# Layer b's attention with each head's rows in its own strip of 32 partitions

## The reference

```python
x = x + attn_a(layernorm(x), ...)     # latent K/V, 16 heads of 8, a rotary part of 32
x = x + ffn(layernorm(x), ...)        # 8 experts, top-k per expert
x = x + attn_b(layernorm(x), qkv_weights)
x = x + ffn(layernorm(x), ...)

def attn_b(x, qkv_weights):           # 16 heads of 8, causal
    q, k, v = ...                     # from x @ qkv_weights
    a = einsum('aib,ajb->aij', q, k) / sqrt(8)
    a = softmax(tril * a + -1e9 * (1 - tril))
    return einsum('aij,ajb->aib', a, v)
```

## Time and profile before

| | us |
|---|---|
| time, median of 3 runs | 1124.67 (1121.18 to 1125.11) |
| the profiled execution's own time | 1126.51 |
| its span | 1124.8 |
| mean granted clock of TensorE | 0.929 |
| PE busy / PEld / DVE / ACT / POOL | 982.4 / 666.7 / 745.9 / 696.5 / 228.6 |
| layer b's attention, first product to last transpose | 613.8 to about 907 |

### The profile page before, as it was taken

How to read it: one execution, slowest core, us unless ns; L and a number is a source line. 1 busy time by engine, 2 the same in 40 slices (tenths; PEclk the granted TensorE clock), 3 DMA queues, 4 the chain that set the end, 5 groups by cost and what they waited for, 6 DMA issues and landing times. The chain is left out here.

```text
span 1124.8 us, 15534 instructions
## 1 busy us (share of the span) xinstructions
PE 982.4 (87%) x5476; PEld 666.7 (59%) x5476; DVE 745.9 (66%) x1305; ACT 696.5 (62%) x1163; POOL 228.6 (20%) x488
## 2 busy tenths in 40 slices
PE   1676999999998799989966799999999859998997
PEld 1344565555554577868844455555655447776886
DVE  6565677767751667669872666766767266776996
ACT  1403566666666589868832066666666748986885
POOL 5103445553342000000007022222222200000000
PEclk9956999999999699989988599999999969998999
DMA  3593432443111011365405521222100020116551
GB/s 83 124 241 82 105 90 83 113 113 86 48 40 57 28 38 38 67 156 145 86 0 142 102 29 30 30 29 30 22 9 1 2 75 19 57 36 134 157 125 39
DMA packets 64957, 81.32 MB, mean 72 GB/s; under 512 B 6080, under 2 KB 52976, under 8 KB 64112
## 3 DMA queue, kind: packets, MB, share of 16 engines
q1 hardware_dynamic: 62944, 79.20, 28.8%
q10 hardware_dynamic: 1936, 1.13, 0.4%
HBM read 56.58 MB, written 22.68 MB: 70 GB/s over the span
## 5 line engine op out<-in xcount | busy, mean ns | idle before, releaser
L1158 PE MATMUL f_banks<-f_hr,f_w2r 128*128 128x512 f32 x768 | 194.1, 401 | 10.3 <-DMA f_w2r<-scratch_w 7.7
L1220 ACT ACTIVATE f_h<-f_banks,b_t 128x512 f32<-128x512 f32 x256 | 167.2, 682 | 44.7 <-PE f_banks L1142 42.0
L1142 PE MATMUL f_banks<-f_xr,f_w1r 128*128 128x512 f32 x768 | 193.0, 400 | 0.0
L1273 DVE TENSOR_TENSOR f_hr<-f_h,f_hr 128x1024 fp32r<-128x1024 f32 x128 | 156.2, 1223 | 31.7 <-ACT f_hr L1226 29.9
L904 DVE TENSOR_REDUCE a_mlate<-a_banks 128x2 f32<-128x1024 f32 (+3 forms) x120 | 124.8, 1079 | 68.2 <-PE a_banks L772 52.1
L1158 PEld LDWEIGHTS f_banks<-f_hr,f_w2r 128*128 128x128 f32 x768 | 144.9, 193 | 40.4 <-DMA f_w2r<-scratch_w 8.6
L904 DVE TENSOR_REDUCE b_mlate<-b_banks 128x2 f32<-128x1024 f32 (+3 forms) x120 | 124.8, 1079 | 57.1 <-PE b_banks L772 41.5
L1142 PEld LDWEIGHTS f_banks<-f_xr,f_w1r 128*128 128x128 f32 x768 | 145.3, 193 | 29.0
L1226 ACT ACTIVATE f_hr<-f_h 128x1024 fp32r<-128x1024 f32 x128 | 136.0, 1062 | 4.1
L764 PE MATMUL a_banks<-a_k,a_q 120*128 120x512 f32 (+3 forms) x384 | 108.6, 388 | 26.8 <-POOL a_q L680 9.2
L807 PE MATMUL a_banks<-a_q,a_k 121*128 121x512 f32 (+3 forms) x384 | 117.2, 388 | 8.0 <-DMA a_q<-a_mt 6.2
(11 more groups left out here) (218 smaller groups left out, 1107.2 us busy)
## 6 DMA issues: line engine op xcount, KB each, us to landing
scratch_w<-a_tab SPq DMA_DIRECT2D x16, 512.0 KB, 3.0
f_w1r<-scratch_w SPq DMA_DIRECT2D x16, 512.0 KB, 5.4
f_w2r<-scratch_w SPq DMA_DIRECT2D x16, 512.0 KB, 6.1
v<-scratch_gate SPq DMA_DIRECT2D x32, 256.0 KB, 5.3
xt<-scratch_gate SPq DMA_DIRECT2D x32, 256.0 KB, 5.2
a_rot<-in_w SPq DMA_DIRECT2D x16, 256.0 KB, 4.1
scratch_q<-a_q_hl SPq DMA_DIRECT2D x24, 128.0 KB, 2.8
scratch_k<-a_k_hl SPq DMA_DIRECT2D x24, 128.0 KB, 2.8
```

Source lines behind the costliest of these rows:

```text
L1142: last = pe.matmul(h_ps[:, j, :], w1r[e % 2][:, wp, j * P:(j + 1) * P], xr[xp][:, chunk(c)], start=(i == 0), stop=(i == 2))
L1158: last = pe.matmul(y_ps[:, q % 2, :], w2r[e % 2][:, wp, j * P:(j + 1) * P], hr[q % 2][hp][:, j, :], start=(j == 0 and i == 0), stop=(j == ...
L1220: act.activation(h[q % 2][:, j, :], h_ps[:, j, :], ACT.Gelu, bias=m.b1_t[:, e * HB + j:e * HB + j + 1]).then_inc(gelu_done, 1)
L1273: dve.tensor_tensor(hr[q % 2][1][:, first:end, :], h[q % 2][:, first:end, :], hr[q % 2][0][:, first:end, :].bitcast(F32), ALU.subtract).th ...
```

## The change

Layer b gets its own layout. Each head's 24 rows lie in its own strip of 32 partitions (head h of the group from partition 32h on), with the maximum's row behind them, and a buffer is [128, 1024] for four heads. No zero rows are multiplied. There are eight buffers each for Q and K, one for each group, and four semaphores for their loads (WAYS); a group's load is 8 DMAs of 24 rows. Products of heads in different strips use different row groups of the array. The pieces of both layers are formed as pairs of heads in two banks; the piece of four heads (`quarter`) in layer b runs in two steps of two heads, each with its own masks, and PE waits for the end of the first step before the second (`fenced`). K in layer b is stored in all three slots like Q. `pt` has buffers of its own in layer b, so ACT's waits for the stores go. SP stores batch 1 not in the projection but in `attention_stage.sync` at half 0, behind the maxima rows of half 1, and loads groups 2 and 3, then (when the stores have landed) 4, and later 5, 6 and 7.

```diff
+WAYS = 4
+KB = len(QSLOT) * HD
+def pieces_early(kind):
+    low = lambda h: ([([(h, 2, 0, 384, 0, 0), (h + 1, 2, 0, 384, 1, 0), (h, 0, 0, P, 0, 384), (h + 1, 0, 0, P, 1, 384)],
+                       [(0, 256, P), (1, 256, P)])],
+                     [("two", 0, 384, h, 2), ("two", 384, P, h, 0)])
+    full = lambda h: ([([(h, 3, 0, CH, 0, 0), (h + 1, 3, 0, CH, 1, 0)], [(0, 384, 0), (1, 384, 0)])],
+                      [("two", 0, CH, h, 3)])
+    return [low(0), full(0), quarter(kind, 1, 0, "four"), low(2), full(2)]
+def quarter(kind, q, k0, how):
+    products = [(h, q, k0, 256, h // 2, h % 2 * 256) for h in range(GH)]
+    if kind == "a":
+        steps = [(products, [(0, P, 256), (1, P, 256)])]
+    else:
+        steps = [(products[i::2], [(bank, P + 256 * i, 0) for bank in range(2)]) for i in range(2)]
+    return steps, [(how, 0, 256, 0, q)]
+def pieces_late(kind):
...
+    near = lambda h, q: pair(h, q, 0, [])
+    ends = lambda h: pair(h, 7, CH, [(0, 384, 0), (1, 384, 0)])
...
+    return [near(0, 7), ends(0), tails(0), near(0, 4), near(0, 5), near(0, 6), quarter(kind, 5, CH, "four"),
+            near(2, 7), ends(2), tails(2), near(2, 4), near(2, 5), near(2, 6)]
 def load_group(eng, m, kind, n, loaded):
+    if kind == "b":
+        for side, t in (("k", m.k2[n]), ("q", m.q2[n])):
+            for h in range(GH):
+                eng.dma_start(t[VW * h:VW * h + KB, :].bitcast(F32),
+                              m.scratch[side][n, :, :, h * T:(h + 1) * T].rearrange("s d t -> (s d) t")
+                              ).then_inc(loaded[n % WAYS], 16)
+        return
 # project_stage
-            for i in range(NBUF):
-                link(pool.memset(m.k2[i][:, :, :].bitcast(F32), 1.0))
-                link(pool.memset(m.q2[i][0:R2, :, :].bitcast(F32), 0.0))
+            for t in m.k2:
+                link(pool.memset(t[:, :].bitcast(F32), 1.0))
 # project_stage.sync
+        store_q(sp, 0, range(1, NG), stored_q[0])
+        store_k(sp, 0, range(1, NG), stored_k[0])
         if latent:
+            second_batch(sp)
         sp.wait_ge(stored_q[0], 16 * stores_q[0])
         sp.wait_ge(stored_k[0], 16 * stores_k[0])
         load_group(sp, m, kind, 1, loaded)
+    def second_batch(sp):
+        sp.wait_ge(split, per * NCH)
+        store_q(sp, 1, range(NG), stored_q[1])
+        store_r(sp, 1, stored_k[1])
+        store_k(sp, 1, range(NG), stored_k[1])
 # attention_stage
+        pt = [sb(f"pt_{i}", [P, GH, CH], F32) for i in range(NPT)]
+    def head_rows(t, n, h, columns, with_max):
+        if latent:
+            return t[n % NBUF][0:M0 + with_max, h, columns]
+        return t[n][VW * h:VW * h + KB + with_max, columns]
 # attention_stage.sync
             if i + 1 < NH2:
                 m_rows(sp, i + 1)
+            if i == 0 and not latent:
+                before.second_batch(sp)
+                load_group(sp, m, kind, 2, loaded)
+                load_group(sp, m, kind, 3, loaded)
+                sp.wait_ge(before.stored_q[1], 16 * before.stores_q[1])
                 sp.wait_ge(before.stored_k[1], 16 * before.stores_k[1])
-            if i == LAST[n] and n + NBUF < GROUPS:
+            if not latent:
+                for g in range(WAYS):
+                    if i + 1 == max(FIRST[g], 1):
+                        load_group(sp, m, kind, g + WAYS, loaded)
 # max_piece
+            for step, (products, masks) in enumerate(PIECES[kind][c][x][0]):
+                if step:
+                    fences[0] += 1
+                    last.then_inc(fenced, 1)
+                    pe.wait_ge(fenced, fences[0])
+                for h, q, k0, w, bank, col in products:
+                    last = pe.matmul(to[:, bank, col:col + w], head_rows(q2, n, h, slice(q * P, (q + 1) * P), 0),
+                                     head_rows(k2, n, h, slice(k0, k0 + w), 0), start=True,
+                                     stop=k0 + w != (q + 1) * P, skip_group_check=True)
```

More of the change, by code:

```diff
@@ L63, in set_tiles @@
     return out, col
[L66 to L74, removed]
@@ L77, in pieces_late @@
[L77 to L88, removed]
@@ L93 @@
+PIECES = {kind: [pieces_early(kind), pieces_late(kind)] for kind in "ab"}
+TURN = [(j, len(PIECES["a"][c])) for j, (n, c) in enumerate(HALVES)]
 LEAD = 17000
@@ L205, in loads_of @@
     buffer_groups = range(n % NBUF, n + 1, NBUF)
-    return sum(3 if kind == "b" else 4 if g and rope_load(kind, g) else 2 for g in buffer_groups)
+    return 2 * GH * (n // WAYS + 1) if kind == "b" else sum(4 if g and rope_load(kind, g) else 2 for g in buffer_groups)
 def rope_load(kind, n):
@@ L349, in load_group @@
                           ).then_inc(loaded[n % NBUF], 16)
[L350 to L356, removed]
+        eng.dma_start(t[R2:M0, :, :].bitcast(F32), m.scratch[side][n, :, :, :].rearrange("s d (h t) -> (s d) h t", h=GH)
+                      ).then_inc(loaded[n % NBUF], 16)
 def rope_copies(n):
@@ L585, in project_stage @@
         stage.free, stage.rope_in = (rot_all, tab_all), rope_in
-    stage.copied, stage.split, stage.splits = copied, split, per * NCH
+    stage.copied, stage.split, stage.splits, stage.second_batch = copied, split, per * NCH, second_batch
     return stage
@@ L754, in max_piece @@
             if x == 0 and j == FIRST[n]:
-                pe.wait_ge(loaded[n % NBUF], 16 * loads_of(kind, n))
+                pe.wait_ge(loaded[n % (NBUF if latent else WAYS)], 16 * loads_of(kind, n))
                 if rope_load(kind, n):
@@ L868, in scalar @@
         m_rows(act, 0)
-        for b in range(B):
+        for b in range(B if latent else 0):
             act.wait_ge(before.stored_q[b], 16 * before.stores_q[b])
@@ L955, in project_and_attend @@
 def project_and_attend(nc, ctx, m, a, kind):
-    loaded = [ctx.enter_context(nc.semaphore(f"loaded_{kind}{i}")) for i in range(NBUF)]
+    loaded = [ctx.enter_context(nc.semaphore(f"loaded_{kind}{i}")) for i in range(NBUF if kind == "a" else WAYS)]
     with ExitStack() as local:
         sb = lambda name, shape, dt: local.enter_context(nc.sbuf_tensor(f"{kind}_{name}", shape, dt))
-        m.q2, m.k2 = [[sb(f"{side}2_{i}", [P, GH, T], F32R) for i in range(NBUF)] for side in "qk"]
+        shape, count = ([P, GH, T], NBUF) if kind == "a" else ([P, T], GROUPS)
+        m.q2, m.k2 = [[sb(f"{side}2_{i}", shape, F32R) for i in range(count)] for side in "qk"]
         m.q_hl, m.k_hl = sb("q_hl", [P, 2, B * T], F32R), sb("k_hl", [P, 2, B * T], F32R)
```

133 lines of the change are left out of this document (61 added, 72 removed).

## The result

The changed kernel takes 1188.7 us (median of 4 runs, 1181.8 to 1192.5) against 1122.9 for the kernel before beside it (4 runs, 1121.1 to 1125.1): a ratio of 1.058, 95% interval 1.052 to 1.063, +65.8 us. The forecast was 1123.5 with a range of 1100 to 1148, so the time lies far outside. The profiled execution took 1189.5 us, its span is 1187.8, its mean granted clock 0.840 (0.929 before).

A forecast was written before the change was run, and what follows sets the result against it. PE was taken to set the pace, though not alone. From 1126.5 us profiled, -8.2 for the steady part and +7.0 for SP's queue gave 1125.3; the runs' median being 1.8 lower, 1123.5 us, range 1100 to 1148.

The forecast's parts named there:

- the rival "the clock": Layer b's steady part: emptier PE falls to clock 0.50, +13 us a group, +85 for all; chance 0.05.
- the steady part and its edges: Layer b's attention, 6.5 head groups: -1.8 us a group on PE, 0.7 of it reaching the end, makes -8.2 us.
- the rival in which nothing runs side by side: Layer b's products: no overlap while strips drain, +4.3 us per group, 1151.3 us in all; chance 0.17.
- The price s of a change of strips: Layer b on PE: each change between strips and full height and back costs 0.25 us, 16 per group, 4.0 us.
- the rival with free strips: Layer b on PE: entering strips costs nothing, -5.8 us per group, 1105.3 us in all; chance 0.29.
- The factor 0.7: Layer b's steady part: 0.7 of each microsecond off PE reaches the end, the rest is paid back in waits.
- PE's sum of -1.8 us per group: Layer b's head group on PE: +0.66 us from pieces and turns, -2.5 from score units.
- term of -2.5 us for units beside their neighbours: Layer b's 40 score units per group run beside the next unit or other heads' pieces: -2.5 us, ends 0 and 5.
- The quarter: Layer b's four-head piece in two steps: 0.64 us, including 0.15 for the wait, plus two strip changes.
- SP's queue: Stores and loads ahead of half 2's maxima rows on SP delay them to 686.0: +7.0 us, start's gain included.
- the stall rival: SP's rows of half 2 come 9 to 10 us late, PE's gain and loss cancel: 1134 us; chance 0.13.
- Start: Layer b's start: pairs, fewer pauses and shorter memsets save 2.0 us, eight loads cost nothing; first maxima's row at 648.4.

The follow-up runs named there:

- the run with 24 rows: Kernel before the change, layer b's products contracting only the 24 (25) rows that aren't zero, all heads in the same rows: 1279.2 us, ratio 1.135.
- full height: Changed kernel with layer b's products of maxima and scores contracting all 128 partitions, summing over four heads: 1134.9 us, ratio 1.0085.
- the mixture with full units: Changed kernel with only the score units contracting 128 partitions, the maxima's pieces still in strips: 1134.2 us, ratio 1.0091.
- the repeated masks: Changed kernel with every mask matmul of layer b's maxima issued four times (1181.9 us, ratio 1.0488) or eight times (1220.9 us, ratio 1.0849).
- split loads: Kernel before the change with each group's three loads cut by head into twelve: 1120.6 us, ratio 0.9954.
- 56 rows: Kernel before the change, layer b's products contracting partitions 64 to 119 (120), 32 of the rows zero: two runs, 1182.9 and 1211.2 us, no ratio given.
- the padded kernel: Kernel before the change with K in strips, Q zero outside its head's strip, products over 127 and 128 rows, loads in 12 DMAs: 1120.7 us, ratio 0.9953.

## Why the prediction was wrong

**The step that failed is the clock: the sum took the steady part at 1.00 and had no term for it, and the rival "the clock" got 0.05.** Instead of the -8.2 us forecast for the steady part and its edges, the stretch between the first and the last copy and the tail took 69.2 us more, at clocks of 0.66 and 0.60. The rival's price, +13 us a group and +85 for all, came near the +9.3 a group (42.31 against 33.06) and +65.8 measured, but by luck: it was for 0.50 throughout. At 0.66 its count of streaming gives 23.3/0.66 = 35.3 us, only 2.3 more than 33. The rival let only the streaming grow with the clock, while in the run with 24 rows the whole group grew with it (33.06/0.64 = 51.7, measured 52.6). Both arguments against it were wrong. That 882 to 908 kept 1.00 with PE busy 21.75 of 26 us was a statement on matmuls of 121 and 128 rows, which was all the trace had; the changed products have 24 and 25, and no row of it showed such a matmul in a steady stretch. And "a slower PE fills itself up again" took PE's busy share for what holds the clock: it did fill up, to 212.89 of 218 us, and stayed at 0.65. The Trainium skill (TensorE: Matmul & The Clock Gate, What's actually happening) has the clock follow how busy PE has recently been; read as the profile's busy share, that rule would keep 1.00 here and in the kernel at 24 rows, where PE is busy 149.79 of 150 us. The traces don't agree: 0.65 and 0.64. I had listed "PEclk below 0.9 between 660 and 880" as what would prove me wrong, but weighed the case by the drain of PE in one stretch (632 to 644) and not by what was new in the instructions themselves.

**Do two products run side by side?** Yes. At the lower clock four matmuls of the kernel after, units and pieces of four heads, start within 0.01 us, and at 1.00 a pair:

```profile
781.69 0.79 PE L842 MATMUL b_banks<-b_q,b_k 25*128 25x512 f32 x1
781.69 0.80 PE L797 MATMUL b_banks<-b_k,b_q 24*128 24x512 f32 x2
781.70 1.21 PE L842 MATMUL b_banks<-b_q,b_k 25*128 25x512 f32 x2
...
784.98 0.50 PE L797 MATMUL b_banks<-b_k,b_q 24*128 24x512 f32 x2
```

The step was right, and the rival in which nothing runs side by side falls.

**The price s of a change of strips.** 0.25 us taken; beside full height 0.27 at the one place measured, so the rival with free strips falls. That it fits is in part luck: s was read as time above the streaming, and by that measure the strips cost 0.43 us and full height, which I had at next to nothing, 0.16; the two errors cancel. I had a loss of 0.66 us per group from the pieces with 16 changes, 0.46 of it in the pace (x 0.7); the mixture with full units, which has the pieces in strips and changes on both sides of each, shows +0.35 in the pace. The factor 0.7 isn't tested by itself.

**PE's sum of -1.8 us per group** can't be read, because no run of the changed schedule was at 1.00 throughout. The estimates from the repeated masks, 28.9 to 32.9 us, lie on both sides of the forecast's 31.8 (33.05 - 1.8 x 0.7). Its term of -2.5 us for units beside their neighbours isn't confirmed: where only the units are in strips, a group at 1.00 takes 2.9 us more, but there the pieces are no partners for them.

**The quarter.** Its wait was costed at 0.15 us; at full height it costs 0.40, which makes 0.8 us a group. In strips the whole quarter takes 1.08 us at 1.00, by the run with full units, where the sum had 0.64 + 2 x 0.25 = 1.14. So the piece was priced about right and the wait alone too low.

```profile
763.29 0.39 PE L801 MATMUL b_banks<-b_k,b_q 24*128 24x256 f32 x2
...
764.37 0.48 PE L846 MATMUL b_banks<-b_q,b_k 128*128 128x512 f32 x1
```

**SP's queue.** +7.0 us forecast, rows landing at 686.0, with the unit at 679.0 before. In the kernel after the term is 0, since half 1 grew by 4 us. At full height it is +8.8 to 9.8 and the unit starts at 682.48, which stands against a start some 2.6 us earlier; half 2 follows 8.7 us late (690.25 - 671.31 = 18.9 us, 10.2 before). So the mechanism was right, and the stall rival's "9 to 10 us" the better size; it hid under the larger loss. The loads occupied the queue for 1.6 to 2.5 us a side, 11.4 us for three groups (665.35 to 676.73), where I had 5.8 a group: I overstated them, and understated that PE gets there sooner.

**Start.** -2.0 forecast; the first product came 4.3 us earlier and the first maxima's row was asked for at 644.1 instead of 648.4. I had costed the eight loads at nothing beside "a transfer of 9 us of unchanged size"; as eight DMAs instead of three, the same bytes were there 2.9 to 3.4 us sooner behind the first issue (6.5 us against 9.4 to 9.9). The split loads show 2.0 to 2.5 us of that for the cut alone.

**Layer a's order of pieces** costs nothing, as forecast.

## What to carry to other kernels

Before work is taken off a matmul by using fewer rows, look for a stretch of the trace in which matmuls of that height alone run for long, and read its granted clock; if there is none, give the lower clock a real chance: PE's busy time didn't show it coming here, and it cost some 69 us where packing was to gain 8. Rows of zeros can be worth their place: 96 of 120 rows here compute nothing, and without them the clock fell from 1.00 to 0.64. And count a pair in strips together with the way in and out of it (0.21 us gained, 0.27 paid): between neighbours at full height it didn't pay here.

## What the runs showed of the hardware that I hadn't expected

- The same schedule at 120 rows, 56 and 24 ran with a granted clock of 1.00, 0.77 and 0.64 between 700 and 850, with PE busy 143.8, 149.2 and 149.8 of 150 us (56 rows: the longer of two runs). Zeros in the rows are no reason for the lower clock: the kernel before multiplies 96 rows of zeros, the padded kernel 103 in Q, and both stay at 1.00.
- Work added to a PE that is the bottleneck can shorten the kernel: 12288 columns of masks a group more, and the group went from 42.3 to 40.7 us, since the clock rose from 0.66 to 0.86.
- The same 24-partition loads, cut from 3 DMAs into 12, brought the first product from 9.9 us (9.4 in two other profiles) to 7.5 us behind the first issue, though twelve take 4.4 us to issue.
- What stays open: what a group of the changed schedule would take at 1.00 throughout; how the rows in use and the time in which they are used together set the clock, of which the runs show only cases; and why the score units' strips lower the clock (0.94) and the pieces' don't (1.00), with equal columns. The units' own pace is lower, so more of their time is spent in strips, but no run separates that from their order.
